# GNN layer with residual and layer norm: first chunk of edges 60 columns instead of 50, third 35 instead of 45, later chunks prepared two steps later

## The reference

```python
edge_in = jnp.concatenate([h[row], h[col], dist], axis=1)
e = jax.nn.silu(edge_in @ eW1 + eb1)
e = jax.nn.silu(e @ eW2 + eb2)
agg = jax.ops.segment_sum(e, row, num_segments=h.shape[0])
node_in = jnp.concatenate([h, agg], axis=1)
out = jax.nn.silu(node_in @ nW1 + nb1) @ nW2 + nb2
...
x = _layernorm(x + out)
```

## Time and profile before

| | us |
|---|---|
| median of 3 runs (lowest, highest) | 623.13 (621.78, 625.88) |
| the profiled execution, its own time | 627.26 |
| its span in the profile | 625.4 |
| PE busy | 564.0 (90%) |
| DVE busy | 426.7 (68%) |
| ACT busy | 367.5 (59%) |
| POOL busy | 428.8 (69%) |

### The profile page before, as it was taken

How to read it: one execution, slowest core, us unless ns; L and a number is a source line. 1 busy time by engine, 2 the same in 40 slices (tenths; PEclk the granted TensorE clock), 3 DMA queues, 4 the chain that set the end, 5 groups by cost and what they waited for, 6 DMA issues and landing times.

```text
span 625.4 us, 15760 instructions
## 1 busy us (share of the span) xinstructions
PE 564.0 (90%) x4943; PEld 482.6 (77%) x4943; DVE 426.7 (68%) x1307; ACT 367.5 (59%) x832; POOL 428.8 (69%) x463
## 2 busy tenths in 40 slices
PE   5987799889999999999999999989997888979795
PEld 4765687868888898888878877878876777769674
DVE  7977889896879678777786877787643442223346
ACT  6375574545745666765655665555556666556554
POOL 2337775677777777777777777777777777777740
PEclk9797889899989999998999999999999899999998
DMA  5312211111112122222222222122222222221111
GB/s 121 104 25 51 56 51 45 39 52 51 52 49 52 51 55 55 55 53 52 56 53 56 52 54 55 52 55 54 54 54 53 54 55 53 56 53 55 52 39 53
DMA packets 17219, 34.23 MB, mean 55 GB/s; under 512 B 8133, under 2 KB 9352, under 8 KB 17017
## 3 DMA queue, kind: packets, MB, share of 16 engines
q0 software_dynamic: 14080, 28.86, 17.5%
q1 hardware_dynamic: 2748, 4.20, 2.5%
q10 hardware_dynamic: 314, 0.16, 0.1%
HBM read 30.73 MB, written 2.40 MB: 53 GB/s over the span
## 4 chain that ended last, share of the span: by engine, by line
POOL 39%; PE 29%; issue 16%; DVE 11%; ACT 2%; DMA 1%; DVEq 1%; ACTq 0%; POOLq 0%
POOL q_rows L818 39%; PE layer_ps L831 13%; PE sort_ps L831 8%; PE seg_ps L831 6%; DVE load_hot L1365 2%; DVE count L1213 1%; DVE agg L1436 1%; PE turn_ps L980 1%; DMA q_rows<-q_table,q_index 1%; DVE col_hot L1359 1%; DVE row_hot L1360 1%; ACT p_table L601 1%; DVE hot L1421 1%; DVEq L1428 1%; PE turn_ps L831 0%
## 5 line engine op out<-in xcount | busy, mean ns | idle before, releaser
L818 POOL DMA_INDIRECT q_rows<-q_table,q_index x440 | 419.1, 953 | 157.3 <-issue 129.9
L670 ACT ACTIVATE e<-layer_ps 128x512 f32<-128x512 f32 x110 | 65.7, 597 | 200.0 <-PE seg_ps L831 195.8
L1436 DVE TENSOR_TENSOR agg<-agg,seg_ps 128x125 f32 x416 | 93.6, 281 | 118.5 <-PE seg_ps L831 115.4
L831 PE MATMUL layer_ps<-hotT,p_table 128*128 128x128 bf16 x1320 | 160.9, 227 | 0.1
L831 PE MATMUL layer_ps<-ident_f,q_rows 128*128 128x128 f32 x440 | 128.5, 292 | 29.7 <-DMA q_rows<-q_table,q_index 28.1
L831 PEld LDWEIGHTS layer_ps<-hotT,p_table 128*128 x1320 | 124.4, 100 | 22.3 <-issue 1.2
L831 PE MATMUL seg_ps<-hot,e 128*128 128x125 f32 x880 | 123.6, 284 | 5.6 <-DVE agg L1436 5.6
L831 PE MATMUL layer_ps<-w_sb,h 128*128 128x128 f32 x880 | 123.9, 285 | 0.0
L831 PEld LDWEIGHTS layer_ps<-w_sb,h 128*128 128x128 f32 x880 | 112.2, 196 | 4.6
L831 PEld LDWEIGHTS seg_ps<-hot,e 128*128 128x128 f32 x880 | 108.5, 194 | 7.5 <-issue 5.5
L831 PEld LDWEIGHTS layer_ps<-ident_f,q_rows 128*128 128x128 f32 x440 | 64.3, 146 | 40.1 <-DMA q_rows<-q_table,q_index 37.3
(11 more groups left out here) (209 smaller groups left out, 472.2 us busy)
## 6 DMA issues: line engine op xcount, KB each, us to landing
q_rows<-q_table,q_index POOLq DMA_INDIRECT x440
q_table<-q_in_sb SPq DMA_DIRECT2D x1, 896.0 KB
x_sb<-in_x_dram SPq DMA_DIRECT2D x1, 700.0 KB
q_table<-q_in_sb SPq DMA_DIRECT2D x1, 504.0 KB
out_dram<-x_sb SPq DMA_DIRECT2D x2, 224.0 KB
out_dram<-x_sb SPq DMA_DIRECT2D x1, 252.0 KB
w_in<-in_edge_weight_dram SPq DMA_DIRECT2D x1, 185.9 KB
dst_i<-in_dst_dram SPq DMA_DIRECT2D x1, 185.9 KB
```

The lines of the kernel that those rows point to most:

```text
L670: A.activation(e2[:, m % 2, :], e_of(m)[:], ACT.Silu).then_inc(e2_ready, 1)
L818: P.indirect_dma_start(q_rows[:, g % RING, j, :], None, q_table, bass.IndirectOffsetOnAxis(ap=q_index[:, GT * g + j:GT * g + j + 1], axis= ...
L831: return nc.tensor.matmul(o, lhsT, rhs, start=start, stop=stop, **kw)
L1436: D.tensor_tensor(o, o, seg_ps[:, j * LO:(j + 1) * LO], ALU.add).then_inc(agg_added, 1)
```

## The change

`LOAD` becomes `[60, 30, 35, 50, ...]`. Chunk 0 then has ten batches of six columns instead of eight and one of two, 84 tile columns instead of 74, and covers groups 0 to 7; chunk 1 (30 columns, as before) covers up to group 15; chunk 2 has six batches instead of eight and 84 tile columns instead of 94, and covers up to group 23 as before. Chunk 0's SPREAD needs a fourth fill, in a free part of `const_ps`. `TURN_SLOT`, `SPREAD_SLOT` and `PLACE_SLOT` go from 5, 9, 12 to 9, 11, 13. `turn(2)`, `pick(1)` and DEST of chunk 1 go ahead of `first_layer(0)`. Chunks 3 and 4 have all parts two steps later, and READ of chunk 2, MATCH of chunk 3, and SCAN with TOTAL of chunk 3 now have steps 9, 10 and 11 in place of step 9 alone.

```diff
-LOAD = [50, 30, 45, 50, 50, 50, 50, 50, 50]
+LOAD = [60, 30, 35, 50, 50, 50, 50, 50, 50]
...
-    at(TENSOR, 1, (CLOSE, 1, 0), (SPREAD, 2, 2))
+    at(TENSOR, 1, (CLOSE, 1, 0))
...
-    sorts(2, [5, 6, 6, 7, 7, 8, 8, 8], [6, 6, 7, 7, 8, 8, 8, 8])
+    sorts(2, [5, 6, 6, 7, 7, 8], [6, 6, 7, 7, 8, 8])
...
-    at(VECTOR, 9, (READ, 2, 0), (MATCH, 3, 0), (SCAN, 3, 0), (TOTAL, 3, 0))
-    at(TENSOR, 9, (OFFSET, 3, 0))
...
-    sorts(3, [11, 12, 12, 13, 13, 14, 15, 15, 16], [12, 13, 13, 14, 14, 15, 16, 16, 17])
...
+    at(VECTOR, 9, (READ, 2, 0))
+    at(VECTOR, 10, (MATCH, 3, 0))
+    at(VECTOR, 11, (SCAN, 3, 0), (TOTAL, 3, 0))
+    at(TENSOR, 11, (OFFSET, 3, 0))
...
+    sorts(3, [13, 14, 14, 15, 15, 16, 17, 17, 18], [14, 15, 15, 16, 16, 17, 18, 18, 19])
...
-    sorts(4, [22, 22, 23, 23, 24, 25, 25, 26, 27], [23, 23, 24, 24, 25, 26, 26, 27, 28])
+    sorts(4, [24, 24, 25, 25, 26, 27, 27, 28, 29], [25, 25, 26, 26, 27, 28, 28, 29, 30])
...
-TURN_SLOT, SPREAD_SLOT, PLACE_SLOT = 5, 9, 12
+TURN_SLOT, SPREAD_SLOT, PLACE_SLOT = 9, 11, 13
...
-                return [(0, [spread_at(flat_ps[0], 0, 4)]), (4, [spread_at(flat_ps[1], 0, 4)]), (8, [spread_at(turn_ps, 0, 2)])]
+                return [(0, [spread_at(flat_ps[0], 0, 4)]), (4, [spread_at(flat_ps[1], 0, 4)]), (8, [spread_at(turn_ps, 0, 2)]), (10, [spread_at(const_ps, 192, 2)])]
...
-            return (rows_read, m + 1) if m <= TIGHT else (pre_ready, m - TIGHT)
+            return (rows_read if m else step_ready, max(m, 1)) if m <= TIGHT else (pre_ready, m - TIGHT)
...
-                first = first_layer(m)
-                first.then_inc(pre_ready if m > TIGHT else rows_read, 1)
-                if m + 2 < GROUPS:
+                if m == 0:
+                    turn(2).then_inc(hotT_ps_ready, 1)
+                    pick(1)
+                    part(DEST, 1, 0)
+                last = first_layer(m)
+                if m:
+                    last.then_inc(pre_ready if m > TIGHT else rows_read, 1)
+                if 1 <= m < GROUPS - 2:
                     last = turn(m + 2)
...
-                if m == 0:
-                    pick(1)
-                    part(DEST, 1, 0)
```

More of the change, by code:

```diff
@@ L49 @@
 TABLE = 512
-CMAX, NMAX, BATCH = max(COLS), max(LOAD), 6
+CMAX, NMAX, NREST, BATCH = max(COLS), max(LOAD), max(LOAD[1:]), 6
 V = 4
@@ L123, in plan @@
     at(TENSOR, 8, (CLOSE, 2, 0), (SPREAD, 3, 2))
-    at(VECTOR, 9, (READ, 2, 0), (MATCH, 3, 0), (SCAN, 3, 0), (TOTAL, 3, 0))
-    at(TENSOR, 9, (OFFSET, 3, 0))
[L126 to L131, removed]
-    sorts(3, [11, 12, 12, 13, 13, 14, 15, 15, 16], [12, 13, 13, 14, 14, 15, 16, 16, 17])
[L133 to L145, removed]
-    sorts(4, [22, 22, 23, 23, 24, 25, 25, 26, 27], [23, 23, 24, 24, 25, 26, 26, 27, 28])
-    at(TENSOR, 28, (CLOSE, 4, 0))
-    at(VECTOR, 29, (READ, 4, 0))
+    at(VECTOR, 9, (READ, 2, 0))
+    at(VECTOR, 10, (MATCH, 3, 0))
+    at(VECTOR, 11, (SCAN, 3, 0), (TOTAL, 3, 0))
+    at(TENSOR, 11, (OFFSET, 3, 0))
+    at(VECTOR, 12, (OFFSET, 3, 0), (SUM, 3, 0))
+    at(TENSOR, 12, (PICK, 3, 0), (DEST, 3, 0))
+    at(VECTOR, 13, (SLOTS, 3, 0), (DEST, 3, 0))
+    at(TENSOR, 13, (WINDOW, 3, 0))
+    at(VECTOR, 14, (WINDOW, 3, 0))
+    at(TENSOR, 14, (CARRY, 3, 0))
+    sorts(3, [13, 14, 14, 15, 15, 16, 17, 17, 18], [14, 15, 15, 16, 16, 17, 18, 18, 19])
+    at(TENSOR, 17, (SPREAD, 4, 0))
+    at(TENSOR, 18, (SPREAD, 4, 1))
+    at(TENSOR, 19, (CLOSE, 3, 0), (SPREAD, 4, 2))
+    at(VECTOR, 20, (READ, 3, 0), (MATCH, 4, 0))
+    at(VECTOR, 21, (SCAN, 4, 0), (TOTAL, 4, 0))
+    at(TENSOR, 21, (OFFSET, 4, 0))
+    at(VECTOR, 22, (OFFSET, 4, 0), (SUM, 4, 0))
+    at(TENSOR, 22, (PICK, 4, 0), (DEST, 4, 0))
+    at(VECTOR, 23, (SLOTS, 4, 0), (DEST, 4, 0))
+    at(TENSOR, 23, (WINDOW, 4, 0))
+    at(VECTOR, 24, (WINDOW, 4, 0))
+    at(TENSOR, 24, (CARRY, 4, 0))
+    sorts(4, [24, 24, 25, 25, 26, 27, 27, 28, 29], [25, 25, 26, 26, 27, 28, 28, 29, 30])
+    at(TENSOR, 30, (CLOSE, 4, 0))
+    at(VECTOR, 31, (READ, 4, 0))
     for k in range(5, CHUNKS):
@@ L395, in win_t_ps @@
             if k:
-                return flat_ps[1][0:NMAX, 64 * (k - 1):64 * k].bitcast(BF16)[:, 0:EP]
+                return flat_ps[1][0:NREST, 64 * (k - 1):64 * k].bitcast(BF16)[:, 0:EP]
             return turn_ps[0:NMAX, 448:512].bitcast(BF16)[:, 0:EP]
@@ L467, in turn_done @@
         def turn_done(g):
-            return (hotT_ps_ready, g + 1) if g < 2 else (step_ready, g - 1) if g - 2 <= TIGHT else (hotT_ps_ready, g - TIGHT)
+            return (hotT_ps_ready, g + 1) if g < 3 else (step_ready, g - 1) if g - 2 <= TIGHT else (hotT_ps_ready, g - TIGHT + 1)
         def table(t, t0, n, width):
@@ L636, in _ @@
                     act.wait_ge(win_t_ready, 2)
-                    A.activation(win_t[:, 1:CHUNKS, :], flat_ps[1][0:NMAX, :].bitcast(BF16)
+                    A.activation(win_t[0:NREST, 1:CHUNKS, :], flat_ps[1][0:NREST, :].bitcast(BF16)
                                  .rearrange("q (k e) -> q k e", e=128)[:, 0:CHUNKS - 1, 0:EP], ACT.Copy).then_inc(win_turned, 1)
@@ L847, in turn_windows @@
                 for k in chunks:
-                    last = nc.tensor.transpose(win_t_ps(k), win_b[:, COL0[k]:COL0[k] + NMAX], ident_b[0:EP, 0:EP])
+                    last = nc.tensor.transpose(win_t_ps(k), win_b[:, COL0[k]:COL0[k] + (NREST if k else NMAX)], ident_b[0:EP, 0:EP])
                 last.then_inc(win_t_ready, 1)
@@ L904, in _ @@
             pe.wait_ge(column_sel_ready, 1)
-            for i in range(3):
+            for i in range(len(spread_fills(0))):
                 spread_windows(0, i)
```

## The result

| | before | after |
|---|---|---|
| median, us (lowest, highest; runs) | 623.62 (620.98, 626.22; 20) | 619.76 (618.35, 623.1; 20) |
| ratio of runs side by side, 95% interval | | 0.9941 [0.9925, 0.9958] |
| the profiled execution, its own time | 627.26 | 619.9 |
| its span | 625.4 | 618.1 |

What follows compares the result with a forecast made beforehand. POOL's gathers bound the kernel: start of the first gather, 550 us, stalls and a tail. For the median run, 627.26 - 11.5 + 4.4 = 620.2, plus 1.0 of stall, gave 621.2 us, range 618.3 to 625.8.

Steps and rivals of the forecast that it cites:

- I take its stalls as 11.5 - 4.1 = 7.4: POOL's stalls in a median run: the profile's 11.5 us less the 4.1 by which the median run was shorter.
- can win back at most the 7.4: The change pays 4.4 us for certain and gains at most the 7.4 us of stalls of a median run.
- Term 1: DVE's work on 60 columns up to READ of chunk 0: first gather 4.4 us later, bounds 3.5 and 6.
- Term 2, PICK of chunk 1 ahead: PICK ahead of group 0: DVE's 2.86 us wait falls under 0.5; 1.0 us gained, bounds 0 and 2.4.
- Term 2, chunk 2 and the later steps: PE's lead: 3.0 us from chunk 2, 1.5 to 3.3 from step 9, 2 x 1.56 from steps without a sort.
- Of step 9: READ, MATCH and SCAN spread out: PE's 2.49 us wait falls to about 1, lower clock's 1.8 shrinks; 1.5 to 3.3 saved.
- two times 1.56: Chunk 4's sort ends in step 30, not 28: PE gains 1.56 us on POOL in each of two steps without sort.
- The clock: PE's second lower-clock stretch, 172 to 176, not counted on for the median: 1.8 us of stall with it, 0 without.
- DVE's burst at step 28: Rival, chance 0.2: chunk 4's sort meets chunk 5's MATCH and SCAN in steps 27 and 28, costing 4.3 us; 625.3.
- PE's gain is smaller: Rival, chance 0.2: DVE's batches in steps 12 to 17 turn PE's chunk 2 savings into waits; 622.2 to 624.2 us.
- the first gather is later by less: Rival, chance 0.07: PE's lag and small steps cover more; start +2.5 to +3.5, no stall, 618.3 to 619.3 us.
- the clock in the prologue: Rival, chance 0.08: PE's clock falls in chunk 0's late batches; first gather 0.8 us later, 622 to 624 us.

Runs made afterwards that it cites:

- e5: The changed kernel with a ring of six groups instead of four (a layer-norm scratch moved to make room): 618.83 us, ratio 0.9929.
- e4: The kernel before with a ring of six groups instead of four (a layer-norm scratch moved to make room): 613.61 us, ratio 0.9854.
- e2: The kernel before with only chunks 3 and 4 two steps later and READ, MATCH, SCAN in steps 9, 10, 11: 617.17 us, ratio 0.9913.
- e7: The kernel before with only READ of chunk 3 and chunk 4 from MATCH on two steps later: 620.88 us, ratio 0.9962.
- e6: The kernel before with the later steps of chunks 3 and 4 and a ring of six groups: 614.28 us, ratio 0.9855.
- e8: The kernel before with the later steps of chunks 3 and 4 and PICK of chunk 1 ahead of group 0: 617.79 us, ratio 0.9908.
- e10: The kernel before with only turn(2), PICK and DEST of chunk 1 ahead of group 0's first layer: 624.99 us, ratio 1.003.
- e11: The changed kernel with turn(2), PICK and DEST of chunk 1 back behind group 0's first layer, run again for its profile: 620.89 us, ratio 0.9961.
- e3: The changed kernel with turn(2), PICK and DEST of chunk 1 back behind group 0's first layer: 620.2 us, ratio 0.9954.
- e1: The changed kernel with chunks 3 and 4, and step 9, back at the steps of before: 628.12 us, ratio 1.0092.

## Why the prediction was nearly right

**The bound held.** The end is the start of the first gather, some 550 us at POOL's pace, the stalls and the tail. After: 44.69 + 552.0 + 0.75 of stalls = 597.4, and the tail of 20.7 makes it 618.1. The medians split into a start of +5.2 (e5 less e4) and stalls of -8.9 (9.8 less the 0.9 that after still loses). That the two give -3.7 is no test, since the same four medians stand on both sides. The test is that the start has a second source, the first gathers of the profiles, and agrees: 38.8 in the mean of the seven with the prologue of before (37.88 to 39.51), 44.1 in the mean of the four with 60 columns (43.42 to 44.69), 5.3 apart.

**Two errors stood against each other.** The forecast was 621.2. The start cost 0.8 more than forecast, the stalls paid 2.5 more (8.9 against 7.4 less 1.0), and the result is 1.4 under the forecast (the kernel before, too, has 623.62 in 20 runs, not 623.13). That the number came out this near is luck in part.

**The step that failed: "I take its stalls as 11.5 - 4.1 = 7.4".** The reason given was that the fixed part cannot shrink. It does differ from run to run. e2, e4 and e7 have the prologue of before, and in their profiles the first gather starts at 37.9; in that of before and in e6, e8 and e10 it starts at 39.5. That is up to 1.6 of the 4.1, and 0.7 against the mean of the seven. PE's clock at the start of chunk 0's sort goes with it. Stretches of before, then of e4:

```profile
20.00:22.00 2.00, 2.00 (x6) 0.50 0.23 74
22.00:24.00 2.00, 2.00 (x7) 0.58 1.00 311
```

```profile
20.00:22.00 2.00, 2.00 (x8) 0.76 0.50 152
22.00:24.00 2.00, 2.00 (x13) 1.00 1.03 328
```

A further 0.7 is the tail (21.5 against 20.6 to 21.0 in the others), and 0.4 to 1.1 the gathers themselves (552.9 without the stalls, against 551.8 to 552.5). So 1.8 to 3.4 of the 4.1 us lay outside the stalls, and the stalls of a median run were near those of the profile. An estimate from four runs says the same: what a kernel gained by its ratio plus the stalls left in its profile is 9.5 (e2: 5.4 and 4.05), 9.7 (e7: 2.4 and 7.3), 10.0 (e4: 9.1 and 0.9) and 9.3 (e6: 9.0 and 0.3). The interval of e4 puts the sum at 8.1 to 11.9, above 7.4. The statement that the change "can win back at most the 7.4" fell with it.

**Term 1, the later start: right in kind, 0.8 too small.** Forecast +4.4, measured 5.2 in the profiles and 5.2 between e4 and e5. The period of a batch was forecast as 1.905 and is 1.91. That PE has caught up by the tenth batch held: READ waits 1.12 in all four profiles with 60 columns, where it waited 2.74. In the two profiles shown the sum missed the steps ahead of the sort, forecast at 1.7 and measured at 2.5: DVE waits for PE's OFFSET (0.44) and for PICK (1.72, before 1.03). PE's matmuls of PICK grow with the columns as well, 24 instead of 20, and the term counted DVE's work alone. Over all the profiles the miss splits otherwise. The sort starts 2.0 later (22.7 against 20.7 in the mean; the wait for PICK is 0.88 in e11 and 1.24 in e5), and READ's wait falls by 1.1 (from 2.2 in the mean), where the term took 1.8.

**Term 2, PICK of chunk 1 ahead: the wait was wrong, the gain is open.** Forecast 1.0 gained (bounds 0 and 2.4) and a wait for PICK of under 0.5. The wait is 2.00 in after (timeline of DVE and of PE):

```profile
57.41 0.19 DVE L1270 TENSOR_SCALAR tile<-sort_ps 125x30 f32<-125x30 f32 x1 [2.00 <-PE sort_ps L833]
```

```profile
54.08 2.63 PE L833 MATMUL sort_ps<-seg_sel,count 125*125 125x5 f32 x12
```

The part on ACT's copy of the spread held: 1.02 us of wait, forecast 1.4. It is the price of PICK that failed. The term took PICK to end 0.5 behind SUM, and PICK takes 2.63 us at the lower clock instead of 1.70. What the edit is worth hangs on the kernel round it. Alone it costs 1.6 us (e10), with the later steps it is worth nothing (e8), and in the change 0.4 to 1.2 (e3, e11), which the forecast's 1.0 fits. The bound of 0 below was too kind: a loss had no reason against it.

**Term 2, chunk 2 and the later steps: right, and larger than priced.** Together they were to leave 1.0 us of stall, and 0.75 is left in the profile, 0.9 in the median. The first part came as forecast. PICK and the smaller chunk 2 were to gain 1.0 and 3.0 us on PE, and at `first_layer(9)` the change is 4.0 and e1 4.3 ahead of before, counted from the first gather. With PICK back (e11) it is 2.2, so PICK's share was rather more than the 1.0 and chunk 2's rather less than the 3.0, as far as one profile each can tell. It doesn't pay the start by itself: without the later steps (e1) the change loses 4.7. The later steps were to gain 1.5 to 3.3 and two times 1.56, and they win 6.2 alone (e2; 5.4 by the ratio), of which 2.8 are chunk 4's (e7), near its two times 1.56. Of step 9 the wait was saved (2.49 to 0.42), and the 1.8 us of lower clock were not in the change: that stretch stands at 126 to 130. What the chunk sizes do in the whole change, with PICK and the slots, is to take away the stalls up to group 13 (3.9 in e2, 0 in after), at a price of 5.2.

**The clock.** Counting the second stretch off for the median run was reasonable but empty: it stayed (0.50 in 178 to 180) and no stall of weight followed it, as PE had the lead by then. That it can come or go is borne out: e2, e5 and e11 have no lower clock between 160 and 220. Its 1.8 us are more than the third that the prediction gives them: 0.6 of the 3.0 between 619.5 and 622.5.

**The rivals.** DVE's burst at step 28 did not come: no stall of the change is longer than 0.45 above the issue time, none above 0.01 stands behind group 31, and from 190 to 230 us PE has no wait for DVE above 0.25. "PE's gain is smaller" and "the first gather is later by less" are out by the same rows, and the clock in the prologue stayed at 1.00 through the last batches (42 to 48).

## What to carry to other kernels

Where one engine issues transfers at a fixed pace into a ring and another empties it late for a while, price the ring's depth before the order of the work: here two more slots took away what three edits of the order took away, and cost no later start. A larger first piece buys slack later at its full price now (5.2 us here), so it pays only if nothing cheaper gives that slack. An edit that gains on one base can lose on another (PICK ahead: 0.4 to 1.2 us gained by the medians and ratios, or 1.6 lost), so price it on the base it will stand in. Do not scale the stalls of a profile down to the median by what that execution took longer: look in profiles of kernels with the same beginning whether the start and the tail differ too.
